# Graph layer, edge stage: the weight matrix keyed by half groups (16 destinations, 8 classes of 160 columns), and GpSimd's transfers laid out anew over the four slots of a group

## What is computed

```python
h = relu(layernorm(x))
f = concat(h[src], h[dst], edge_attr)             # 40000 x 1088
m = mish(mish(f @ W1 + b1) @ W2 + b2)             # one message per edge
agg = segment_sum(m, dst)                         # 1250 x 512
x = x + LN(h + mish(concat(h, agg) @ W3 + b3) @ W4 + b4)
h = relu(layernorm(x))
s = (h @ U * s) @ Vt
x = x + relu(segment_sum(s[src] * edge_weight, dst) + bias)
```

## Time and profile before

| | us |
|---|---|
| median of 3 runs | 1604.23 (1601.88 to 1606.79) |
| the profiled execution, its own time | 1601.37 |
| its span in the trace | 1599.7 |
| PE busy | 1539.2 (96%) |
| DVE busy | 1453.3 (91%) |
| ACT busy | 1307.5 (82%) |
| POOL busy | 1117.6 (70%) |
| mean granted PE clock | 0.987 |

### The profile page before, as it was taken

The page is one execution under the profiler, slowest core; times in us unless marked ns, Lnnn a source line. Parts: engine busy times, 40 slices in busy tenths (PEclk is TensorE's granted clock), DMA queues, the critical chain, the costliest instruction groups (busy, mean ns, idle before and its releaser), DMA issues.

```text
span 1599.7 us, 32991 instructions
## 1 busy us (share of the span) xinstructions
PE 1539.2 (96%) x7870; PEld 1183.6 (74%) x7870; DVE 1453.3 (91%) x3139; ACT 1307.5 (82%) x2503; POOL 1117.6 (70%) x989
## 2 busy tenths in 40 slices
PE   6759999999999999999999999999999999999998
PEld 5537777777777777777777777777777777776785
DVE  6538999999999999999999999999999999995676
ACT  2218999989989999999999989899999999985462
POOL 3036788888888888878888888888888888862220
PEclk9879999999999999999999999999999999999999
DMA  8743444444445445445444444444444454455564
GB/s 297 258 148 99 118 119 115 124 112 121 120 110 125 121 107 130 117 109 125 117 113 120 118 112 121 117 115 119 118 115 123 112 122 121 108 138 127 119 141 158
DMA packets 109666, 205.08 MB, mean 128 GB/s; under 512 B 30377, under 2 KB 41001, under 8 KB 109632
## 3 DMA queue, kind: packets, MB, share of 16 engines
q0 software_dynamic: 48736, 119.55, 32.9%
q1 hardware_dynamic: 60896, 85.12, 17.0%
HBM read 151.52 MB, written 42.83 MB: 121 GB/s over the span
## 4 chain that ended last, share of the span: by engine, by line
PE 85%; DVE 5%; issue 2%; ACT 1%; DMA 0%; DVEq 0%; POOL 0%; ACTq 0%; POOLq 0%
PE bm L959 52%; PE bp L944 6%; PE bp L946 6%; PE bs L982 5%; PE bp L948 4%; PE pm L970 3%; PE pm L969 3%; PE pu L1836 1%; PE po L1858 1%; PE pu L330 1%; PE pu L1903 1%; DVE bm L1122 1%; PE pu L1890 0%; DVE rp L1094 0%; DVE tp L1103 0%
## 5 line engine op out<-in xcount | busy, mean ns | idle before, releaser
L874 POOL TENSOR_TENSOR hTl<-tp,hTh 128x512 fp32r<-128x512 f32 (+1 forms) x316 | 407.3, 1289 | 206.6 <-DVE kl L1131 196.6
L959 PE MATMUL bm<-W2h,hTh 128*128 128x512 f32 x1252 | 506.4, 404 | 2.6 <-DVE bm L1122 2.6
L959 PE MATMUL bm<-W2l,hTh 128*128 128x512 f32 x1252 | 495.3, 396 | 0.0
L959 PE MATMUL bm<-W2h,hTl 128*128 128x512 f32 x1252 | 495.0, 395 | 0.0
L857 POOL DMA_INDIRECT xg<-A_tab,idx x309 | 327.9, 1061 | 61.2 <-issue 54.3
L959 PEld LDWEIGHTS bm<-W2h,hTh 128*128 128x128 f32 x1252 | 235.1, 188 | 90.0 <-DVE bm L1122 24.4
L959 PEld LDWEIGHTS bm<-W2l,hTh 128*128 128x128 f32 x1252 | 235.3, 188 | 56.7
L959 PEld LDWEIGHTS bm<-W2h,hTl 128*128 128x128 f32 x1252 | 235.5, 188 | 49.2
L1094 DVE SCALAR_TENSOR_TENSOR rp<-rp 128x512 f32<-128x512 f32 (+1 forms) x316 | 239.1, 757 | 27.6 <-ACT rp L1015 27.1
L1015 ACT ACTIVATE rp<-bp 128x512 f32<-128x512 f32 (+1 forms) x316 | 186.0, 589 | 80.9 <-PE bp L948 76.5
L1018 ACT ACTIVATE rp<-rp 128x512 f32<-128x512 f32 (+1 forms) x316 | 196.8, 623 | 48.9 <-DVE rp L1094 48.9
(11 more groups left out here) (217 smaller groups left out, 2453.0 us busy)
## 6 DMA issues: line engine op xcount, KB each, us to landing
ea<-in_eaT SPq DMA_DIRECT2D x156, 128.0 KB
M_tab<-mev POOLq DMA_DIRECT2D x79, 160.0 KB
agg_tab<-ev POOLq DMA_DIRECT2D x157, 64.0 KB
db<-in_dst_rows SPq DMA_DIRECT2D x78, 128.0 KB
M<-M SPq DMA_DIRECT2D x78, 128.0 KB
M_tab<-zero POOLq DMA_DIRECT2D x10, 640.0 KB, 21.2
eaW<-Bh_tab SPq DMA_DIRECT2D x79, 64.0 KB
eaW<-Bl_tab SPq DMA_DIRECT2D x79, 64.0 KB
```

Source lines behind the costliest of these rows:

```text
L874: e.tensor_tensor(hTl[p][:, j, 0:w], tp[u.const % 2][:, 0:w], hTh[p][:, j, 0:w], ALU.subtract)\
L959: last = e.matmul(bank[0:r, :], a[p][:, c, j * P:j * P + r], w[:, c, :], start=False, stop=c == KC - 1 and w is W2l, skip_group_check=True)
```

## The change

M's half groups become the unit. Each half of a group (2 tiles, 256 edges) gets a window of its own of 16 destinations, and the sources are in 8 classes of 160 columns, so there are still 128 keys (16 x 8). PE's two matmuls have 160 columns and write the left half of `pm` for the first two tiles, the right half for the others. ACT still copies 320 columns. POOL adds them to `M_tab` in two transfers of 128 rows x 160, at two bases that it loads from `base_i`, which now has three numbers for each group. DVE makes `so` with 160 columns, and one `khl` of 2 x 128 elements in place of `kh` and `kl`: one scalar_tensor_tensor in place of two tensor_scalars. `low` now waits for the second of two counts. On POOL a gather moves from slot 0 to slot 3, and the second half's transfer goes into slot 0. The setup stage computes the half windows (`windows`, `bases`, `columns`). The last stage reads the same bytes of `M_tab` in the same layout.

```diff
+EQ = 8
+EC = NP // EQ
+EWIN = 16
+KEYS = EQ * EWIN
+HSUB = SUB // 2
...
-    win_d = dram("win_tab", (NG, 2))
-    M_d = dram("M_tab", (NP * Q, QC))
+    win_d = dram("win_tab", (NG, 4))
+    M_d = dram("M_tab", (NP * EQ, EC))
...
-                        c_v.inc(e.tensor_reduce(win[:, 0:1], dsti[:, :], AX.X, ALU.min))
-                        link(e.tensor_reduce(mx[:], dsti[:, :], AX.X, ALU.max))
+                        halves = dsti[:, :].rearrange("g (h n) -> g h n", h=2)
+                        c_v.inc(e.tensor_reduce(win[:, 2:4], halves, AX.X, ALU.min))
+                        link(e.tensor_reduce(mx[:], halves, AX.X, ALU.max))
+                        c_v.inc(e.tensor_reduce(span[:, 2:3], mx[:], AX.X, ALU.max))
+                        link(e.tensor_scalar(win[:, 2:4], win[:, 2:4], float(NP - EWIN), None, ALU.min))
+                        c_v.inc(e.scalar_tensor_tensor(span[:, 0:2], mx[:], float(WIN - EWIN), win[:, 2:4], ALU.add, ALU.subtract))
+                        link(e.tensor_reduce(win[:, 0:1], win[:, 2:4], AX.X, ALU.min))
                         link(e.tensor_scalar(win[:, 0:1], win[:, 0:1], float(NP - WIN), None, ALU.min))
-                        link(e.tensor_tensor(win[:, 1:2], mx[:], win[:, 0:1], ALU.subtract))
+                        link(e.tensor_tensor(span[:, 2:3], span[:, 2:3], win[:, 0:1], ALU.subtract))
+                        link(e.tensor_reduce(win[:, 1:2], span[:], AX.X, ALU.max))
...
-                        c_v.inc(e.tensor_copy(base_i[0:1, :], base_b[0:1, :, 0]))
+                        ints = base_i[0:1, :].rearrange("a (g k) -> a g k", k=3)
+                        c_v.inc(e.tensor_copy(ints[:, :, 0:1], base_b[0:1, :, 0:1]))
+                        c_v.inc(e.tensor_copy(ints[:, :, 1:3], base_b[0:1, :, 2:4]))
...
-                        c_v.inc(e.scalar_tensor_tensor(kcol[:], drel[:], float(Q), rem[:], ALU.mult, ALU.add))
+                        link(e.tensor_tensor(kcol[:].rearrange("p (g h s) -> p g h s", h=2, s=HSUB),
+                                                dcol[:].rearrange("p (g h s) -> p g h s", h=2, s=HSUB),
+                                                base_b[:, :, 2:4].rearrange("p g (h s) -> p g h s", s=1)
+                                                .to_broadcast([P, NG, 2, HSUB]), ALU.subtract))
+                        c_v.inc(e.scalar_tensor_tensor(kcol[:], kcol[:], float(EQ), rem[:], ALU.mult, ALU.add))
...
-                        link(e.tensor_scalar(rem[:], scolf[:], float(QC), None, ALU.is_ge))
-                        for r in range(2, Q):
-                            link(e.scalar_tensor_tensor(rem[:], scolf[:], float(r * QC), rem[:], ALU.is_ge, ALU.add))
-                        c_v.inc(e.scalar_tensor_tensor(scol4[:], rem[:], -float(QC), scolf[:], ALU.mult, ALU.add))
-                        c_v.inc(e.tensor_tensor(wcol_l[:], wcol[:], wcol_h[:], ALU.subtract))
+                        link(e.tensor_scalar(scoli[:], scolf[:], float(-(-2 ** 19 // EC)), None, ALU.mult))
+                        link(e.tensor_scalar(scoli[:], scoli[:], 19, None, ALU.arith_shift_right))
+                        link(e.tensor_copy(rem[:], scoli[:]))
+                        c_v.inc(e.scalar_tensor_tensor(scol8[:], rem[:], -float(EC), scolf[:], ALU.mult, ALU.add))
+                        c_v.inc(e.tensor_tensor(wcol_hl[:, :, 1], wcol[:], wcol_hl[:, :, 0], ALU.subtract))
...
-                        e.dma_start(M_d[i * P * Q:(i + 1) * P * Q, :].rearrange("(p r) n -> p r n", p=P),
-                                    zero[:, :, 0:QC].to_broadcast([P, Q, QC])).then_inc(q_z, 16)
+                        e.dma_start(M_d[i * P * EQ:(i + 1) * P * EQ, :].rearrange("(p r b) n -> p r (b n)", p=P, b=2),
+                                    zero[:, :, 0:2 * EC].to_broadcast([P, EQ // 2, 2 * EC])).then_inc(q_z, 16)
...
-                                        row_bcast(win_d.rearrange("g a -> (g a)"), 2 * NG, P)).then_inc(q_winb, 16)
+                                        row_bcast(win_d.rearrange("g a -> (g a)"), 4 * NG, P)).then_inc(q_winb, 16)
...
-    GATHER_AHEAD = {2: (10, (0,)), 3: (9, (1,)), 0: (8, (2, 3))}
+    GATHER_AHEAD = {2: (10, (0,)), 3: (9, (1, 2)), 0: (8, (3,))}
...
+    ADJ_LAG = {2: (6, 0), 0: (8, 1)}
...
-                    e.wait_ge(v_adj, u.val(3, 3 * (ADJ_AHEAD - DVE_PRE + 1)))
+                    e.wait_ge(v_adj, u.val(2, 2 * (ADJ_AHEAD - DVE_PRE + 1)))
...
-            def adjacency(u, b):
-
-                e.wait_ge(a_adj, u.group(1, 1))
-                wait(e, q_adj, u.group(16))
-                e.dma_start(M_d[bass.ds(b * Q, KEYS), :], mev[u.par][:], accum_op=ALU.add).then_inc(q_adj, 16)
+            def adjacency(u, half):
+
+                b = e.value_load(base_i[0:1, bass.ds(u.group(3, 1 + half), 1)], min_val=0, max_val=NP - EWIN)
+                if half == 0:
+                    e.wait_ge(a_adj, u.group(1, 1))
+                wait(e, q_adj, u.group(32, 16 * half))
+                if half:
+                    e.sem_inc(s_go, 1)
+                e.dma_start(M_d[bass.ds(b * EQ, KEYS), :], mev[u.par][:, half * EC:(half + 1) * EC], accum_op=ALU.add)\
+                 .then_inc(q_adj, 16)
...
-                if q.j == 2 and q.has(4 * FULL):
-                    adjacency(q, held[0])
+                if s.j in ADJ_LAG:
+                    lag, half = ADJ_LAG[s.j]
+                    if (s + -lag).has(4 * FULL):
+                        if half == 0 and s.reg is None and s.const == lag:
+                            e.wait_ge(q_z, 16 * (ZERO_DMAS + NCH))
+                        adjacency(s + -lag, half)
...
-                i, r = u.const % 2, ETAIL if tail(u) else P
+                i, r, half = u.const % 2, ETAIL if tail(u) else P, pm[:, u.j // HSUB * EC:(u.j // HSUB + 1) * EC]
                 if u.j == 0:
                     wait(e, a_adj, u.group())
-                e.wait_ge(v_adj, u.val(3, 3))
-                e.matmul(pm[:, 0:QC], kh[i][0:r, :], so[i][0:r, :], start=u.j == 0, stop=False, skip_group_check=True)
-                e.matmul(pm[:, 0:QC], kl[i][0:r, :], so[i][0:r, :], start=False, stop=u.j == SUB - 1 or tail(u),
+                e.wait_ge(v_adj, u.val(2, 2))
+                e.matmul(half, khl[i][0:r, 0, :], so[i][0:r, :], start=u.j % HSUB == 0, stop=False, skip_group_check=True)
+                e.matmul(half, khl[i][0:r, 1, :], so[i][0:r, :], start=False, stop=u.j % HSUB == HSUB - 1 or tail(u),
...
-                wait(e, q_adj, u.group(16, -16))
-                e.activation(mev[u.par][:], pm[:, 0:QC], ACT.Copy).then_inc(a_adj, 1)
+                wait(e, q_adj, u.group(32, -32))
+                n = EC if tail(u) else 2 * EC
+                e.activation(mev[u.par][:, 0:n], pm[:, 0:n], ACT.Copy).then_inc(a_adj, 1)
...
-                e.tensor_scalar(so[i][0:r, :], iota_q[0:r, :], scol4[0:r, c], None, ALU.is_equal).then_inc(v_adj, 1)
-                e.tensor_scalar(kh[i][0:r, :], iota_k[0:r, :], kcol[0:r, c], wcol_h[0:r, c].bitcast(F32), ALU.is_equal,
-                                ALU.mult).then_inc(v_adj, 1)
-                e.tensor_scalar(kl[i][0:r, :], iota_k[0:r, :], kcol[0:r, c], wcol_l[0:r, c], ALU.is_equal, ALU.mult)\
-                 .then_inc(v_adj, 1)
+                e.tensor_scalar(so[i][0:r, :], iota_q[0:r, :], scol8[0:r, c], None, ALU.is_equal).then_inc(v_adj, 1)
+                e.scalar_tensor_tensor(khl[i][0:r, :, :],
+                                       iota_k[0:r, :].rearrange("p (a k) -> p a k", a=1).to_broadcast([r, 2, KEYS]),
+                                       kcol[0:r, c],
+                                       wcol_hl[0:r, c, :].rearrange("p a (h k) -> p (a h) k", k=1).bitcast(F32)
+                                       .to_broadcast([r, 2, KEYS]), ALU.is_equal, ALU.mult).then_inc(v_adj, 1)
```

More of the change, by code:

```diff
@@ L54 @@
 HALFN = NP // 2
-KEYS = Q * WIN
+EQ = 8
[3 more added lines that the diff above has]
+HSUB = SUB // 2
 SBLK = [(0, HALFN // 2), (HALFN // 2, NPAIR - HALFN // 2)]
@@ L252, in gnn_two_layers @@
         iota_p = sb("iota_p", [P, 1])
-        base_b = sb("base_b", [P, NG, 2])
-        base_i = sb("base_i", [1, NG], I32)
         wide_i = sb("wide_i", [1, 1], I32)
@@ L267, in gnn_two_layers @@
         ev = [sb(f"ev{i}", [2 * WIN, H]) for i in range(2)]
-        mev = [sb(f"mev{i}", [KEYS, QC]) for i in range(2)]
+        mev = [sb(f"mev{i}", [KEYS, 2 * EC]) for i in range(2)]
         st, sb_early, _ = scope()
@@ L333, in gnn_two_layers @@
         est, sb, _ = scope()
+        base_b = sb("base_b", [P, NG, 4])
+        base_i = sb("base_i", [1, 3 * NG], I32)
         W2h = sb("W2h", [P, KC, H], F32R)
@@ L336, in gnn_two_layers @@
         b2b = sb("b2b", [P, H])
-        iota_q = sb("iota_q", [P, QC])
+        iota_q = sb("iota_q", [P, EC])
         iota_k = sb("iota_k", [P, KEYS])
-        scol4 = sb("scol4", [P, NG * SUB])
+        scol8 = sb("scol8", [P, NG * SUB])
         kcol = sb("kcol", [P, NG * SUB])
-        wcol_h = sb("wcol_h", [P, NG * SUB], F32R)
```

(30 more changed lines are left out.)

2 lines of the change are left out of this document (1 added, 1 removed).

## The result

The changed kernel takes 1620.84 us (median of 5 runs, 1616.08 to 1623.33), the kernel before 1604.23 us: a ratio of 1.0099, 95% interval 1.0075 to 1.0123: small, but clear of no change. I had forecast 1583 us. The profiled execution has a span of 1619.2 us, before 1599.7.

What follows compares the result with a forecast made beforehand. PE was taken to bound the edge stage, DVE 0.07 us a tile behind. 1601.37 - 22 (PE) + 1 (setup), DVE and POOL at 0, made 1580.4 us; with 2.9 us to the median, 1583 us, range 1560 to 1604.

Steps and rivals of the forecast that it cites:

- So the lateness costs 0.: POOL's slots: hTl of a group's first two tiles comes late, but what waits for it is not held; 0 us.
- the price of repeated operands: DVE's khl: oh's 421 ns, 0.12 us above the 1 ns line, put on top of khl's lower end, making 0.47 us.
- PE: 22 us forecast: PE's two adjacency matmuls of 160 columns: 0.22 us in place of 0.29, 0.07 us less for each of 313 tiles.
- a floor of 0.11 us under both matmuls: PE's adjacency matmuls: the weight load, not the 160 columns, holds each spacing at 0.11 us.
- no floor: Rival on PE's narrow matmuls: bound only by their columns, 0.08 us each, full 41 us gained, 1563 us; 5%.
- DVE: 0.73 us forecast: DVE's adjacency instructions: so 0.26 plus khl 0.47 us in place of 0.80, 0.07 us less per tile.
- Setup: +1 us forecast: Setup stage: one more cast and subtraction after the base arrives and a larger base transfer add 1 us (0.7 to 2).
- POOL: 0 forecast: POOL in the edge stage: one more transfer of 1.02 us per group fits its idle time and doesn't bound; 0 us.
- 1602: Rival, DVE becomes the bound: khl at its upper bound brings DVE's work to 4.24 us a tile, no change; 7%.
- The slow narrow matmul: Rival on PE: narrow matmuls run slower per column, 0.56 us for 0.29, +85 us, 1687 us; 13%.
- POOL holds the others: Rival: POOL becomes the bound or its late hTl holds others, part of the gain or none, 1594 us; 12%.

Runs made afterwards that it cites:

- the control: The kernel before, with the second operand of DVE's square of rp taken from PSUM (bp) in place of SBUF: 1594.7 us, ratio 0.9943.

## Why the prediction was wrong

**The step that failed** is POOL's: "So the lateness costs 0." I had the slots right in kind (slot 3 overfull, slots 0 and 1 late, slot 2 on time), but the lateness too small: the `hTl` of slot 0 starts 1.4 us after its `khl` (799.45 to 800.89) and that of slot 1 1.0 us after (803.72 to 804.68), where one on time starts after 0.1. I had 0.9 and 0.3 us, from a slot of 4.17 us in the mean, but from this `khl` to the one before it are only 3.9 us; slot 3's work was 5.3 us (5.1 forecast), its second gather 1.47 in place of 1.08. I named those who wait for `hTl` by a semaphore; with the square's operand swapped none of them costs PE a gap. I left out who shares something with it without a semaphore. Before, `hTl` starts right behind `kl`, and the bias copy, the message and `tp` that follow give it 1.8 us in which DVE neither has both inputs of a long instruction in SBUF nor runs in a fast mode (SBUF to SBUF with one tensor input, as the cast: 0.42 us for 512 columns, where the bias copy to PSUM takes 0.68); it needs 1.29. `hTl` uses nothing of `kl`, so its wait, 196.6 us in all, only sets its place. I read it as idle time to be spent. Late by 1 us or more it no longer fits.

I had the rule in hand, from the Trainium skill's page "SBUF — State Buffer" (section "SBUF: two separate sides"): the port pair is held for a whole instruction, by a fast-mode DVE instruction or one with two SBUF inputs, or by POOL. The prediction names only the fast mode and leaves out the two SBUF inputs, which is the square's case. It has `hTl` as the loser, where DVE lost. And I brushed it aside with one row, the `hTl` of slot 1 with 1.32 us in the earlier trace rows. I should have looked at the DVE side: before, the mean square already had 764 ns, against 682 with the swapped operand. The trace agrees with the page: the square stretched to 1.6 us, `kh` to 1.38 us, the copy from SBUF to PSUM never (mean 681 ns after, 680 before).

A second sign stood in my own rows. `oh`, whose 421 ns I took as the price of repeated operands, has two SBUF inputs, and in the kernel before each of its 74 rows between 150 and 1400 us starts under `hTl` and ends 0.14 to 0.16 us after it:

```profile
801.15 0.40 DVE L1084 TENSOR_TENSOR oh<-iota_w,drel 128x128 f32<-128x128 f32 x1
```

The `hTl` of the earlier trace rows ends at 801.41, this row at 801.55. So its length says when `hTl` ended, not what such operands cost; `khl` was measured at 473 ns.

**The sum, term by term.** PE: 22 us forecast; the trace gives (0.29 - 0.185) x 313 = 33 us, and the two runs with the swapped square give 1594.7 - 1560.45 = 34 us. I had put a floor of 0.11 us under both matmuls; only the second shows it, the first is followed after 0.07 us, about the 0.08 of my "no floor" case. DVE: 0.73 us forecast for `so` and `khl`, 0.60 measured (`so` alone 290 ns, below the 335 that I had as its least). Setup: +1 us forecast, 1.7 us less measured (the first L946/L971 starts at 106.9 instead of 108.6 us). POOL: 0 forecast. With 1620.84 - 1560.45 = 60 us for the collisions after, and 9 us before, it is 51 us. 1604 - 34 + 51 = 1621, but this has to close, since the terms are differences of the same four runs; it splits the time and does not check it. The runs with the swap may hold a few us from lighter data; if both hold the same, the control bounds that at 9. Three rivals in the prediction were priced from bases that differ by up to 3 us (1687 should be 1690, 1602 should be 1605, 1563 should be 1564), which changes nothing.

**The rivals.** The slow narrow matmul, which I gave most of the slower side, didn't happen. "POOL holds the others" was the right place with the wrong price: I let it take half of the gain, and it takes one and a half times the gain. It needed a price from DVE's side: squares 109 us more, less the 0.20 x 313 = 63 us of its shorter instructions, less 13 us of shorter casts (484 to 441 ns), 33 us more of work; its busy time grew by 36 (1453.3 to 1489.7). Its idle time in the window fell from 10.2 to 2.2 us in 600, an estimated 18 us over the stage. The rest, 15 to 18 us, is close to the 19.5 us by which the span grew.

## What to carry to other kernels

When an instruction is moved in time, list besides those who wait for it also what runs beside it, on the engine with which it shares a port, at the old time and at the new. A wait that looks idle may be what keeps two engines apart, so look whether the other engine's durations, not its waits, have a second value. And when a slot is filled past its length, what matters is where the overhang ends, not whether the sum still fits in the group.

## What was new about the hardware

A DVE instruction with both tensor inputs in SBUF, or a fast one from SBUF to SBUF, that starts while a POOL tensor_tensor runs gets longer and shows no wait: a square of 0.69 us takes 1.6 us behind one in the change, and 2.1 to 2.9 where two follow each other. It ends a fixed time after POOL's (0.55 to 0.57 us for the square, 0.15 for `oh`), and this is the sign to look for. With one input in PSUM it keeps its length. It also goes the other way: POOL's `hTl` took 1.96 us behind a DVE cast and `so`, and POOL's issue of a gather grows from 1.05 to 2.35 us beside a run of such DVE instructions, while its plain adding transfers stay between 0.9 and 1.5. Of two narrow matmuls in a row, the first is followed after 0.07 us and the second after 0.11 us, while a series of 64 columns keeps 0.115.
